# Block products and value units of a projection loop: one value unit moved one block product later, a value-weight split moved with it

## What is computed

```python
q = hidden_states @ Wq + bq      # 512 -> 32 heads x 128
k = hidden_states @ Wk + bk
v = hidden_states @ Wv + bv
q = rms_norm(q, gq); k = rms_norm(k, gk)
```

## Time and profile before

| | |
|---|---|
| median of the runs | 2332.31 us |
| the profiled execution's own time | 2332.17 us |
| its span, first to last instruction | 2330.4 us |
| mean granted clock of TensorE | 0.988 |
| the projection block in it | about 107 to 650 us |
| busy: PE, DVE, ACT, POOL | 95%, 73%, 53%, 41% |

### The profile page before, as it was taken

One profiled execution on the slowest core, in us unless ns is written; L12 is line 12 of the kernel. 1 busy time (PEld: TensorE's weight loads), 2 busy tenths in 40 slices (PEclk: granted clock), 3 DMA queues, 4 the chain that ended last, 5 costly groups with the idle time before them and its releaser, 6 DMA issues. The chain is left out here.

```text
span 2330.4 us, 34717 instructions
## 1 busy us (share of the span) xinstructions
PE 2222.0 (95%) x10852; PEld 1839.3 (79%) x10852; DVE 1705.1 (73%) x2794; ACT 1236.3 (53%) x2094; POOL 959.0 (41%) x865
## 2 busy tenths in 40 slices
PE   7988999999989999999999999999998999899998
PEld 5767777777768888888888888888886788687887
DVE  5676665565578888888888888888886575785665
ACT  3355544444466666666666666666663343352442
POOL 4486555555522222222222212222213466672565
PEclk9999999999999999999999999999999999999999
DMA  3155545555432212212211221221201121041210
GB/s 113 41 183 185 193 165 173 171 184 164 167 103 82 72 50 81 81 49 73 81 55 66 81 69 53 81 72 50 81 24 41 50 68 44 33 128 37 73 59 36
DMA packets 108487, 210.47 MB, mean 90 GB/s; under 512 B 9984, under 2 KB 42752, under 8 KB 107136
## 3 DMA queue, kind: packets, MB, share of 16 engines
q1 hardware_dynamic: 108416, 209.58, 26.9%
HBM read 140.33 MB, written 69.21 MB: 90 GB/s over the span
## 5 line engine op out<-in xcount | busy, mean ns | idle before, releaser
L1489 ACT ACTIVATE at_pT_hi<-ps 128x512 fp32r<-128x512 f32 x512 | 278.4, 596 | 353.2 <-PE ps L1593 353.1
L1531 DVE TENSOR_REDUCE at_small<-ps 128x1 f32<-128x1024 f32 x256 | 312.7, 1222 | 87.2 <-PE ps L417 86.4
L1541 DVE TENSOR_TENSOR at_pT_lo<-ps,at_pT_hi 128x512 fp32r<-128x512 f32 x512 | 327.3, 681 | 3.7 <-ACT at_pT_hi L1489 3.7
L1496 ACT ACTIVATE at_probs<-ps,at_small,cols 128x1024 f32<-128x1024 f32 x256 | 309.3, 1208 | 28.2 <-DVE at_small L1533 22.2
L1593 PE MATMUL ps<-ident,at_probs 128*128 128x128 f32 x2048 | 266.3, 273 | 3.1 <-DVE at_pT_lo L1541 3.1
L1593 PEld LDWEIGHTS ps<-ident,at_probs 128*128 128x128 f32 x2048 | 239.1, 140 | 37.9 <-issue 4.3
L417 PE MATMUL ps<-ln_xT_hi,first_parts 128*128 128x512 f32 x656 | 222.0, 400 | 7.1 <-DVE ln_xT_lo L288 4.0
L1426 POOL TENSOR_TENSOR at_o_lo<-at_o_raw,at_o_hi 128x512 fp32r<-128x512 f32 x32 | 41.3, 1292 | 439.7 <-ACT at_o_hi L1510 439.7
L417 PE MATMUL ps<-ln_xT_hi,queries 128*128 128x512 f32 x816 | 221.6, 391 | 0.0
L1555 DVE SCALAR_TENSOR_TENSOR x<-ps,at_small,x 128x512 f32<-128x512 f32 x256 | 192.2, 751 | 8.0 <-PE ps L417 3.1
L417 PE MATMUL ps<-ln_xT_hi,ln_xT_lo 128*128 128x512 f32 x768 | 196.0, 390 | 0.0
(11 more groups left out here) (308 smaller groups left out, 5514.1 us busy)
## 6 DMA issues: line engine op xcount, KB each, us to landing
scratch_v<-v_res SPq DMA_DIRECT2D x64, 256.0 KB, 2.3
scratch_q_hi<-qkv_q_hi SPq DMA_DIRECT2D x64, 256.0 KB, 2.4
scratch_q_lo<-qkv_q_lo SPq DMA_DIRECT2D x64, 256.0 KB, 2.7
scratch_k<-qkv_res SPq DMA_DIRECT2D x64, 256.0 KB, 2.4
keys<-scratch_k SPq DMA_DIRECT2D x32, 512.0 KB, 3.5
at_v_raw<-scratch_v SPq DMA_DIRECT2D x32, 512.0 KB, 3.3
wv_raw<-in_Wv SPq DMA_DIRECT2D x8, 1024.0 KB, 5.9
first_raw<-in_Wqk SPq DMA_DIRECT2D x16, 512.0 KB, 4.0
```

Of the source, the lines that this page charges most:

```text
L1489: nc.scalar.activation(pT2[jp][0][:, 4 * b:4 * b + 4, w * P:(w + 1) * P], T_BANKS[:, b * HALF:(b + 1) * HALF].rearrange("p (k n) -> p k n" ...
L1496: nc.scalar.activation(probs[l % 4][:], scores(l)[:], ACT.Exp, bias=nbias[:, l % 4:l % 4 + 1], scale=rq[:, l % NT:l % NT + 1], accum_out=s ...
L1531: nc.vector.reduce_max(maxes[:, l % 4:l % 4 + 1], scores(l)[:], AX.X).then_inc(s_max, 1)
L1541: nc.vector.tensor_tensor(pT2[jp][1][out], T_BANKS[:, b * HALF:(b + 1) * HALF].rearrange("p (k n) -> p k n", k=4), pT2[jp][0][out], ALU.su ...
```

## The change

```diff
-        QUADS, UNITS, EARLY, BODY = 4, 8, 5, 6
+        QUADS, UNITS, EARLY, BODY = 4, 8, 4, 5
...
-        VALUE_PARTS = {1: (0,), 2: (1, 2), 3: (3,)}
+        VALUE_PARTS = {1: (), 2: (0, 1, 2), 3: (3,)}
...
                     if j == 0 and not is_first(g):
-                        for u in range(BODY, UNITS):
+                        for u in range(BODY, UNITS - 1):
                             store_values(g - 1, u)
+                    if j == 1 and not is_first(g):
+                        store_values(g - 1, UNITS - 1)
                         src = ins["bv"][bass.ds(g * HALF, HALF)].partition_broadcast(P)
                         sp.wait_ge(v_res_done, g * UNITS)
                         sp.dma_start(bv[:], src).then_inc(bv_in, 16)
...
                     elif not is_first(g):
                         evict_values(g - 1, BODY + 1)
+                    if j == 1 and not is_first(g):
+                        evict_values(g - 1, UNITS - 1)
                     if j + 1 < QUADS:
                         low_late(g, j + 1)
...
                     times(d_bank(j), j, S1, T1).then_inc(p5_done, 1)
-                    if j == 0 and not is_first(g):
-                        values_unit(g - 1, BODY + 1)
+                    if j < 2 and not is_first(g):
+                        values_unit(g - 1, BODY + 1 + j)
```

## The result

The changed kernel took 2373.94 us (median of 4, 2369.58 to 2377.43) against 2332.76 us for the kernel before on the same chip: ratio 1.0175, 95% interval 1.0153 to 1.0198. It is slower by 41 us; the prediction was 37 us slower, in a range from 2346 to 2383 us. The profiled execution of the changed kernel took 2377.32 us.

The account below looks back on a forecast made before the run. PE is busy 95%, so only its idle time can be won. Tails starting 7.66 us later in 7 groups (53.6 us), less 16.3 us from six shorter tails, give +37.3 us on 2332.17: 2369 us, range 2346 to 2383.

Parts of the forecast that it names:

- The filled wait: Quad 2, groups 1 to 7: the unit moved into quad 1 fills PE's 2.00 us wait for `keep_p1`.
- SP's queue and who waits for it: Quad 1's k store is issued late, at 265.39 instead of 260.27; `evict11` of quad 2 waits for it, 6.24 us later.
- The landing: Quad 1's k store, in a burst behind the bias load, lands at 271.4, with bounds 267.6 and about 1 us above.
- PE's wait for `keep_u2`: Before p7 of quad 2, PE would wait about 3.3 us for `keep_u2` on DVE.
- The third split: From `evict11` to `evict22` of quad 2, one more value-weight split lengthens the chain by 1.42 us a group.
- Rival (b): In every group, longer PE waits also cost TensorE clock, 2.2 us each, 15.6 us more: 2385 us; chance 0.16.
- A period: Sign in the profile after: one group would take 70.1 us, against 65.2 us before.
- What costs nothing: Unit 7's eviction on DVE (0.69 us), the split taken from j = 1 and the next weight load delay nothing PE needs.
- rival (c): Quad 1's k store lands by 265.2 and doesn't bind: -6.4 us, 2326 us; chance 0.08 with the ground between.
- The rule for one DMA: K store's landing by about 2.0 us plus bytes at 436 GB/s: lands at 268.0, total about 2346 us.
- The unit ahead of group 0: Removing the unit ahead of group 0's first quad gains 0, beside PE's 7.67 us wait for ACT; 2.7 us without that cover.

Follow-up runs that it names:

- e1: Changed kernel with the store of unit 7 and the bias load put on SP behind quad 1's k store of C11: 2351.14 us.
- e2: Changed kernel with the bias load alone put behind the k store of C11, the store of unit 7 left in front: 2361.23 us.
- e10: Changed kernel with the eviction of unit 7 put on DVE behind `q_low` of C12, SP's order left as in the change: 2372.72 us.
- e4: Kernel before with `EARLY = 4`, moving unit 4 of group 0 from ahead of the first quad into group 0's tail: 2332.81 us.
- e7: e1 with the eviction of unit 7 put on DVE behind `q_low` of C12 of quad 0: 2325.35 us.
- e11: e9 with the last value-weight split moved from j = 3 to j = 2, so none stands behind quad 3's work: 2294.61 us.
- e12: Kernel before with the value-weight splits of e11 and no unit moved: 2318.63 us.
- e3: Kernel before with one value-weight split moved from j = 1 to j = 2 and nothing else: 2347.60 us.
- e5: Kernel before with two value-weight splits at j = 1, one at j = 2, one at j = 3, and no unit moved: 2326.01 us.
- e9: e7 with two value-weight splits at j = 1, one at j = 2 and one at j = 3: 2312.05 us.

## Why the prediction was right, and where it was off

**The filled wait.** Right. The wait for `keep_p1` is gone from quad 2 in groups 1 to 7.

**SP's queue and who waits for it.** Right, with its place. The store of unit 7 went out at 260.96 (predicted 261.07), the k store at 265.96 (265.39), and `evict11` waited for its landing; e1, e2 and e10 show that the order on SP is a cause. The landing was mis-sized: 4.5 us behind its issue in this group and 3.9 to 4.6 in the seven, `evict11` at 270.5, where I had 271.4, 6.0 us behind the issue. SP issued more slowly in the burst (3.75 us from the first query store to the k store instead of 3.02), and the DMAs drained faster than the 0.71 us each that I took. PE's wait for `keep_u2` was 2.1 us on average, not 3.3.

**The third split.** Right in sum: from `evict11` to `evict22` it is 280.42 - 270.47 = 9.95 us instead of 8.48, 1.47 us more where I took 1.42. Only 3.51 - 2.92 = 0.59 us of this stand in the row of the splits; the rest lies ahead of them, where it is 357.24 - 350.72 = 6.52 us from `evict11` to the first split instead of 5.64. With both, the tail starts 289.74 - 282.95 = 6.8 us later in the group instead of 7.66, which makes 7 x 6.8 - 16.3 = +31 us instead of +37. The missing 0.9 us a group is `evict11`, which came 5.3 us later than in the template and not 6.24.

**The clock.** This is the term missing from the sum. Rival (b) had it at 2.2 us a group with a chance of 0.16, on top of the forecast, and it came in six tails at 5.28 - 2.72 = 2.56 us, 15 us. The kernel before had some 4 us of the same in its two long periods, 67.45 us and 66.86 us. 31 + 15 - 4 = 42 us, against the 45 us between the two profiled executions and 41 us between the medians. A period is 71.99 us where I had 70.1. So the forecast came out near the measurement with one term 6 us too large and another, 11 us net, left out: rival (b) added to a smaller shift. That the two errors nearly cancel is luck. What I had set against rival (b) came from one group: the kernel before is granted 0.50 for about 3 us behind two waits of 2.79 us and behind waits of 2.02 and 1.90 us, in other groups.

**What costs nothing.** One item of that list was incomplete. I followed the eviction of unit 7 on DVE to `low_late` and `evict22`, and not to `q_low` of C12, which stands behind it and feeds the last query store on SP, ahead of the same k store. In the changed kernel this hold lies beside the one on SP, so the sum didn't suffer. But rival (c), the time without SP's hold (2326 us), was wrong for that reason: e1 gave 2351 us, and 2325 us came only with the eviction moved too.

**The rule for one DMA.** The estimate of 2.6 us for 256 KB from the Trainium skill (DMA: Bandwidth & Descriptors, the section on the anatomy of one DMA) gave about 2346 us. In the changed kernel `evict11` followed the issue of that store by 3.9 to 4.6 us, in e2 by 3.0 to 3.8 us, and in e1, where only the last pair of query stores went out in the 5 us before it, by 2.6 us (337.27 - 334.66). The rule agrees with the last and not with the store behind that burst.

**The unit ahead of group 0.** Open: e4 allows anything from 0 to 2.8 us.

## What to carry to other kernels

When an eviction moves to a later place, follow three queues: what stands behind the new wait on its engine, what stands behind its store on the DMA-issuing queue, and what reads the semaphores of all of these; here a k store with 1.7 us of slack was held twice, and undoing either hold alone left the kernel 19 and 39 us slower. Ask what else the move that fills a wait holds up: the same move that cost 41 us was 8 us faster than the kernel before when its store and its eviction stood behind what others wait for (e7), and with no split in the last stretch of the chain it came to 2294.61 us (e11), 1.7% below the kernel before; 0.65% of this the splits alone give (e12). No run has the change with its split put back and both holds left in. Price a longer PE wait with a restart at half clock, too: in e3 that was the greater part of the cost.

## What the runs showed of the hardware

Behind a wait of PE the granted clock of TensorE was often 0.50 for some us. The cost is not only the idle time: a unit of 12 matmuls took 5.28 us instead of 2.72. How long the one wait was doesn't tell whether it happened:

- waits of 4.2 us at the tail in the changed kernel, with three more waits of PE in the 18 us before: about 5 us at 0.50 in six of six, from the first matmul on. Waits of 3.94 to 3.96 us in e3, with one wait of 1.5 us some 19 us before: the same in five of five;
- waits of 3.86 us (the last tail of the changed kernel) and 4.03 us (the first of e3): about 3 us, from 0.7 and 1.3 us behind the restart;
- waits of 3.1 us at the tail in e7: about 3 us in five of five; one of 3.57 us in the same trace: none;
- waits of 2.3 to 2.5 us in quad 2: about 3 us in five of seven in e12, in one of seven in e5;
- waits of 2.8 us at the tail in the kernel before: in two of five, and not at once. Of the one at 348.17 this is the stretch behind it, which begins with the sixth matmul:

```profile
349.52:352.50 2.98, 2.98 (x9) 2.30 (x8) 0.58 (x1) 0.00 (x0) 1.70 (x1) 0.50 0.98 305
```

- waits of 1.6 to 1.9 us at the tail in e9: in one of seven (at 344.9, behind 1.82 us), though all seven tails began with a matmul of 0.49 or 0.50 us. A first matmul at full pace doesn't show that the clock stays up.

What SP had issued ahead of it delayed the landing of the k store. From its issue (256 KB) to the instruction that waits for its landing it took 3.9 to 4.6 us behind a store, the broadcast load of the bias and six stores, 3.0 to 3.8 us without the bias load (e2), and 2.6 us in e1, where only the last pair of query stores had gone out in the 5 us before.
